# A gated cross-attention and FFN layer on one core: x kept in one ring, four PSUM banks in strict turn, normalised rows made later, and the last output projection ahead of the last FFN product

## What is computed

```python
x = x + tanh(g_xattn) * attention(layernorm(x), ctx, ctx)   # causal; projections q, k, v, o with biases
x = x + tanh(g_ffn) * (mx(layernorm(x)) @ mx(weight).T + bias)
```

## Time and profile before

| what | value |
|---|---|
| three runs: median (lowest to highest) | 1426.57 us (1426.28 to 1427.3) |
| the profiled execution | 1426.4 us |
| its span, first to last instruction | 1424.4 us |
| mean granted TensorE clock | 0.989 |
| busy: PE (matmuls), PEld (weight loads) | 1381.7 us (97%), 1220.1 us (86%) |
| busy: DVE (VectorE), ACT (ScalarE), POOL (GpSimd) | 1102.1, 894.7, 854.3 us |

### The profile page before, as it was taken

The page is one execution under the profiler, slowest core; times in us unless marked ns, Lnnn a source line. Parts: engine busy times, 40 slices in busy tenths (PEclk is TensorE's granted clock), DMA queues, the critical chain, the costliest instruction groups (busy, mean ns, idle before and its releaser), DMA issues.

```text
span 1424.4 us, 35124 instructions
## 1 busy us (share of the span) xinstructions
PE 1381.7 (97%) x10844; PEld 1220.1 (86%) x10844; DVE 1102.1 (77%) x4219; ACT 894.7 (63%) x2969; POOL 854.3 (60%) x1387
## 2 busy tenths in 40 slices
PE   6899999999999999999999999999999999999976
PEld 6788888888888888888888888888888888888865
DVE  5778787887788878778788778788778887877763
ACT  4566666666666666666666666666666666666651
POOL 2455665566665666666656566556666566666662
PEclk9999999999999999999999999999999999999988
DMA  8444434444434444434444443444443444443310
GB/s 255 107 112 106 117 93 120 115 128 107 119 90 118 118 125 118 108 94 116 118 119 124 108 114 97 116 117 128 107 119 93 115 117 125 118 111 90 86 51 29
DMA packets 156103, 159.10 MB, mean 112 GB/s; under 512 B 28176, under 2 KB 130576, under 8 KB 155920
## 3 DMA queue, kind: packets, MB, share of 16 engines
q1 hardware_dynamic: 155920, 156.87, 41.6%
HBM read 39.33 MB, written 16.78 MB: 39 GB/s over the span
## 4 chain that ended last, share of the span: by engine, by line
PE 91%; DVE 3%; SPq 2%; issue 1%; ACT 1%; POOL 1%; DMA 1%; DVEq 0%; ACTq 0%; POOLq 0%
PE proj L483 20%; PE proj L484 20%; PE proj L485 20%; PE pT_ps L533 12%; PE oT_ps L550 6%; PE proj L577 6%; PE s_ps L522 4%; PE s_ps L523 2%; SPq L342 1%; DMA all_probs<-in_L_xattn_w_v 1%; ACT all_probs L660 1%; DVE all_probs L807 0%; DMA q_stack<-q_hi 0%; POOL x L448 0%; POOL x L444 0%
## 5 line engine op out<-in xcount | busy, mean ns | idle before, releaser
L410 POOL TENSOR_TENSOR all_probs<-all_probs,rden 128x128 f32<-128x128 f32 (+1 forms) x1024 | 505.0, 514 | 473.3 <-DVE rden L867 472.1
L660 ACT ACTIVATE all_probs<-all_probs,neg_max 128x128 f32<-128x128 f32 (+1 forms) x1024 | 458.7, 451 | 396.7 <-DVE neg_max L807 396.5
L807 DVE CUSTOM_DVE_ANT_0 all_probs<-s_ps,causal 128x128 f32<-128x128 f32 (+1 forms) x1024 | 321.7, 351 | 164.4 <-PE s_ps L523 160.8
L533 PE MATMUL pT_ps<-ident,all_probs 128*128 128x128 f32 x1536 | 264.5, 282 | 6.6 <-POOL all_probs L410 4.3
L660 ACT ACTIVATION_READ_ACCUMULATOR all_probs<-all_probs,neg_max 128x1 f32 x1024 | 195.5, 191 | 0.0
L919 DVE COPY all_probs<-pT_ps 128x384 f32<-128x384 f32 x256 | 139.0, 543 | 66.5 <-PE pT_ps L533 66.5
L533 PEld LDWEIGHTS pT_ps<-ident,all_probs 128*128 128x128 f32 x1536 | 160.4, 142 | 21.7 <-issue 12.7
L522 PE MATMUL s_ps<-k_stack,q_stack 96*128 96x256 f32 x512 | 154.8, 302 | 2.8 <-DVE neg_max L807 2.2
L483 PE MATMUL proj<-cT_hi,wk_hi 128*128 128x256 f32 x512 | 153.2, 299 | 1.9 <-DVE cT_lo L861 1.1
L483 PE MATMUL proj<-aT_hi,wq_hi 128*128 128x256 f32 x512 | 148.0, 289 | 0.4 <-ACT vs L675 0.4
L484 PE MATMUL proj<-cT_lo,wk_hi 128*128 128x256 f32 x512 | 142.4, 278 | 0.0
(11 more groups left out here) (125 smaller groups left out, 3487.3 us busy)
## 6 DMA issues: line engine op xcount, KB each, us to landing
k_stack<-k_hi SPq DMA_DIRECT2D x512, 64.0 KB, 2.0
q_stack<-q_hi SPq DMA_DIRECT2D x512, 64.0 KB, 2.1
xs<-in_x SPq DMA_DIRECT2D x32, 512.0 KB, 4.2
cs<-in_ctx SPq DMA_DIRECT2D x32, 512.0 KB, 6.1
k_stack<-k_lo SPq DMA_DIRECT2D x256, 64.0 KB, 2.0
q_stack<-q_lo SPq DMA_DIRECT2D x256, 64.0 KB, 2.1
out<-x SPq DMA_DIRECT2D x32, 512.0 KB, 3.0
vs<-in_L_xattn_w_k SPq DMA_DIRECT2D x2, 512.0 KB, 7.0
```

The costliest lines, as they stand in the source:

```text
L410: last = nc.gpsimd.tensor_tensor(p, p, rden[:, sd, t, h:h + 1].to_broadcast([P, (1 + t) * P]), ALU.mult)
L533: last = nc.tensor.transpose(pT_ps[h % 2][:, m * P:(m + 1) * P], probs[:, h % P_RING, m * P:(m + 1) * P], ident[:, :])
L660: last = nc.scalar.activation(probs[:, h % P_RING, cols], probs[:, h % P_RING, cols], ACT.Exp, scale=-1.0, bias=neg_max[:, sd, t, h:h + 1] ...
L807: last = nc.vector.tensor_tensor_reduce(probs[:, h % P_RING, cols], s_ps[h % 2][:, cols], causal[:, (1 - t) * P:], 1.0, MASKED, ALU.add, A ...
```

## The change

It does four things. Lines of the changed kernel differ from those of the profile, so both are given by what they do.

1. **x in one ring.** `xs` has five places, x1 is gone, and the o unit, the FFN bias and the f product all work in the place into which x was loaded. A load of x from batch 5 on waits for the result of the batch five earlier to be written out; loads 2 to 4 wait for the last transposes of weights. The result goes out in two transfers of 256 KB, each when its half of f is added. SyncE's copies of k1 also wait for the maxima of the batch before.
2. **Four banks in strict turn.** All units, and both `weigh_values` of a batch ("av"), take the next of four banks in the order in which TensorE comes to them; each waits for the unit four turns back.
3. **xn later.** The normalised rows of batch i-1 are made in slots 2 and 3 of step i, one half in each, in place of slot 15 of step i-1. Batch 0 keeps its place.
4. **The step of the last o.** In step 34 the order is dT0 (30) in slot 1, the `weigh_values` in slot 3, dT1 (30) and o0 (31) in slot 4, o1 (31) in slot 5, f0 (30) in slot 9 and f1 (30) in slot 10.

```diff
-AV_LAG = 11
-OUT_SLOTS = ((AV_LAG + 1) % SLOTS, (AV_LAG + AV_HEADS + 1) % SLOTS)
+AV_SLOTS = (11, 3)
+AV_STEPS = (2, 3)
-BANKS = (0, 1, 2, 0, 1, 2, 0, 1, 2, 0, 1, 2, 0, 1, 0, 2)
+LAST_O = ((1, ("dT", 0)), (4, ("dT", 1)), (4, ("o", 0)), (5, ("o", 1)), (9, ("f", 0)), (10, ("f", 1)))
+BANKS = 4
-XN_SLOT = SLOTS - 1
-X_RING = 4
+XN_SLOTS = (2, 3)
+X_RING = 5
...
+    for i in range(STEPS):
+        if i == B + 2:
+            for s, (kind, half) in LAST_O:
+                work.setdefault((i, s), []).extend((kind, half, i - lag_of[kind, half], p) for p in range(PARTS[kind]))
...
+        def bank_of(kind, half, b):
+            return proj[place_of[kind, half, b] % BANKS]
+        def bank_before(kind, half, b):
+            n = place_of[kind, half, b] - BANKS
+            return taken[n] if n >= 0 else None
...
@@ SyncE, step
+                    if some(n := HEADS * (i - 2)):
+                        sp.wait_ge(max_ok, n)
                     sp.wait_ge(left["k"], 2 * (i - 2) + 2)
...
-                    if some(n := 2 * i):
-                        sp.wait_ge(xn_ok, n)
+                    if i == 1:
+                        sp.wait_ge(xn_ok, 2)
+                    elif 1 < i < X_RING:
+                        sp.wait_ge(wT_done, KC * len(WEIGHTS))
+                    elif i >= X_RING:
+                        sp.wait_ge(out_moved, 16 * T * (i - X_RING + 1))
...
-                    sp.wait_ge(left["f"], 2 * (i - 4) + 2)
-                    sp.dma_start(batch_of(out, i - 4), x1[:, side(ph, 4), :, :]).then_inc(
-                        x1_moved[side(ph, 4)], 16)
+                    for half in range(T):
+                        sp.wait_ge(left["f"], 2 * (i - 4) + half + 1)
+                        sp.dma_start(out[i - 4, half * P:(half + 1) * P, :], xs[:, place(ph, 4), half, :]).then_inc(
+                            out_moved, 16)
@@ TensorE
+            def free_bank(kind, half, b):
+                before = bank_before(kind, half, b)
+                if before and before[0] == "av":
+                    pe.wait_ge(olo_ok, 2 * before[2] + before[1] + 1)
+                elif before and before[0] == "bias":
+                    pe.wait_ge(add_ok, 1)
+                elif before:
+                    pe.wait_ge(left[before[0]], 2 * before[2] + before[1] + 1)
@@ VectorE
-                    dve.wait_ge(x1_moved[sd], 16 + 8 * b - 8 * sd)
-                    nc.vector.tensor_tensor(x1[:, sd, half, :], bank[:, :], xs[:, pl, half, :],
-                                            ALU.add).then_inc(left["o"], 1)
+                    nc.vector.tensor_tensor(x1[:, half, :], bank[:, :], x1[:, half, :], ALU.add).then_inc(left["o"], 1)
...
+                    if s in XN_SLOTS and i > 1 and live(i - 1):
+                        normal_rows(i - 1, XN_SLOTS.index(s))
```

More of the change, by code:

```diff
@@ L285, in transposed_head, with finished @@
             return lag, i - lag, (s - PT_LAG) % SLOTS
[L287 to L303, removed]
+        def finished(i, s, ago=1):
+            n = SLOTS * i + s - ago
+            for kind, half, b, part in work.get((n // SLOTS, n % SLOTS), ()):
+                if part == PARTS[kind] - 1:
+                    yield kind, half, b
+        def bank_of(kind, half, b):
[3 more added lines that the diff above has]
+            return taken[n] if n >= 0 else None
         block = es.enter_context(nc.Block())
@@ L388, in _ @@
             for_steps(step)
-            for n in range(2):
-                sp.wait_ge(x1_moved[n], 16 + 16 * (B // 2))
+            sp.wait_ge(out_moved, 16 * T * B)
         @block.gpsimd
@@ L554, in weigh_values, with unit @@
                 last.then_inc(av_done, 1)
-            def unit(u, part, kind, half, b, i):
-                bank = proj[BANKS[u]]
-                if part == 0 and (before := bank_before(u, i)):
-                    pe.wait_ge(left[before[0]], before[1])
+            def unit(kind, half, b, part):
+                bank = bank_of(kind, half, b)
+                if part == 0:
+                    free_bank(kind, half, b)
                 if part == 0 and at(b, 0) and kind in WEIGHTS:
@@ L604, in unit @@
                     last.then_inc(done[kind], 1)
-            def units(i, s):
-                for (u, part), its_slot in zip(parts, slot_of):
-                    kind, half, lag = UNITS[u]
-                    if its_slot == s and live(i - lag):
-                        unit(u, part, kind, half, i - lag, i)
             def step(i, ph):
@@ L627, in step @@
                         transpose_probs(b, h)
-                    units(i, s)
+                    for kind, half, of, part in work.get((i, s), ()):
+                        unit(kind, half, of, part)
                     for chunk in weight_chunks(i, s):
@@ L663, in exponentials, with unit @@
                 last.then_inc(p_ok, 1)
-            def unit(u, kind, half, b, sd):
-                bank = proj[BANKS[u]]
+            def unit(kind, half, b):
+                bank = bank_of(kind, half, b)
                 if kind in ("o", "f"):
@@ L674, in unit @@
                         act.wait_ge(av_done, n)
-                    nc.scalar.activation(vs[:, sd, half, :], bank[:, :], ACT.Copy).then_inc(left["v"], 1)
+                    nc.scalar.activation(vs[:, side(b, 0), half, :], bank[:, :], ACT.Copy).then_inc(left["v"], 1)
                 elif kind in ("q", "k"):
@@ L748, in step @@
                                              saturate=False).then_inc(w8_ok, 1)
[L749 to L751 removed]
+                    for kind, half, of in finished(i, s, 6):
+                        if kind == "o":
+                            to_grid(of, half)
             for_steps(step)
@@ L826, in moments, with unit @@
                                         ALU.add).then_inc(va, 1)
-            def unit(u, kind, half, b, pl, sd):
-                bank = proj[BANKS[u]]
+            def unit(kind, half, b):
+                bank = bank_of(kind, half, b)
+                x1 = xs[:, b % X_RING]
                 if kind in ("q", "k"):
```

149 lines of the change are left out of this document (80 added, 69 removed).

## The result

The changed kernel takes 1406.1 us (median of 4 runs, 1405.28 to 1409.21), the kernel before, run beside it, 1426.93 (4 runs). The ratio is 0.9858, 95% interval 0.9841 to 0.9875, so 17.8 to 22.7 us less; the forecast was 20.7 us less, 1405.7 us. The profiled execution took 1405.65 us at a span of 1403.9.

The account below looks back on a forecast made before the run. TensorE was taken as the bound, losing time to VectorE in steady steps and idling at the end. 12.5 + 1.1 + 0.4 + 4.9 + 1.2 + 0.6 = 20.7 off 1426.4 gives 1405.7 us, range 1401 to 1414.

Parts of the forecast that it names:

- Banks and xn, 0.43 a step, 12.5: Steady steps: 0.15 us from cT0's bank wait and 0.28 from k0 behind cT_lo go, 29 times; bounds 4.4 and 19.7.
- cT_lo 0.8 us early: Steady step: with xn moved, cT_lo ends near 676.1, k0 is due at 676.96, so 0.8 us to spare.
- xn hidden in slots 2 and 3: VectorE: xn's halves, the first about 0.8 us, fit its idle times of 1.19 and 1.05 us there.
- Rival D: Slots 2 and 3: xn is in the way, TensorE loses up to 1.59 us a step; 1436.8 us, chance 0.04.
- x in one ring, 0: Summing x in one ring costs nothing while its load is half a step ahead; 0, bounds -1 to 1 us.
- Start, 1.1: Step 2: k0's 1.06 us wait for cT_lo goes, step 3 gains nothing; 1.1 us, bounds 0 and 3.
- Step 32's 0.43, step 33's 0.4 and the order of step 34, 4.9: Steady gain in step 32, q1's wait for v1's bank gone in 33, reordered 34 starting dT0 (31) 4.9 us earlier.
- Tail 1.2 and last transfer 0.6: After last dT0: fewer slow matmuls if the clock stays up, 1.2 us (0 to 2.5); halved last transfer, 0.6 us.
- B: Steady steps: cT_lo stays late through ScalarE's other work, k0 keeps its 0.28 us; 1413.8 us, chance 0.10.
- C: Steady steps keep their length, only start and end gain; 1418.2 us, chance 0.07.
- E: End: the hole before o0 keeps the lower clock through both o halves, 4.8 us more; 1411.7 us, chance 0.07.
- F: Every step: units cycling through banks make the clock swing, 70 us; 1475 us, chance 0.01.

Follow-up runs that it names:

- the xn experiment: Changed kernel with both halves of xn back in slot 15, the four banks in turn kept: 1419.08 us, ratio 0.9945.
- the half xn: Changed kernel with the first half of xn back in slot 15, the second left in slot 3: 1406.03 us, ratio 0.9846.
- its run: Kernel before with only x summed in place in one ring of five, all else taken back: 1427.2 us, ratio 1.0002 (0.9993 to 1.001).
- its repetition: The changed kernel itself, unaltered, run and profiled once more: 1407.06 us, ratio 0.9853.
- the usual order: Changed kernel with the last batch's o behind f of the batch before in step 34: 1412.31 us, ratio 0.9896.
- one transfer: Changed kernel with each batch's result in one transfer of 512 KB instead of two of 256 KB: 1407.38 us, ratio 0.9856.
- the two with another end: Changed kernel with half 1's o and f (30) later in step 34: 1407.64 us; the same with nine f0 products ahead of dT1: 1407.76 us.
- the one with xn four times: Changed kernel with every half of xn computed four times in slots 2 and 3, thrice into a spare tensor: 1484.5 us, ratio 1.0393.
- the double xn: Changed kernel with every half of xn computed twice in slots 2 and 3, once into a spare tensor: 1405.83 us, ratio 0.985.

## Why the prediction was right

The time was 0.4 us from the forecast, on the forecast's own mechanisms, though two of its terms were right only as a sum. That it was as near as 0.4 us is luck: four runs of the same kernel lay 3.9 us apart.

*Banks and xn, 0.43 a step, 12.5.* Measured 0.43 to 0.46 a step and 11.8 us over 28 intervals, the first profile's 1.1 us longer one included. The sum is right, since with both stops gone both holes close. The attribution failed. The step that reads "TensorE loses 0.15 us there", as a price of its own beside xn's 0.28, took two stops on one engine for independent. With xn in slot 15 VectorE goes without a break from k_lo over xn to the maxima, ScalarE's exponentials and cT_hi wait for these, and cT_lo for cT_hi; that chain fixes when k0 can start, wherever cT0 stands. A cT0 set free 0.15 us sooner leaves its gain at k0: its change is worth 0, as the longer wait of the xn experiment shows. Behind a moved xn it is worth 0.21. The lower bound "4.4 if only the bank's wait goes" was wrong by the same reasoning; it should have been 0.

*cT_lo 0.8 us early.* It ends 0.91 us before k0. Where k0 waits for it, it ends 0.14 before (677.25 and 677.39), so 0.77 are spare, and the half xn that moved it by 0.79 used them up.

*xn hidden in slots 2 and 3.* Right, with more room than argued. The prediction carried slot 15's 0.8 us a half along; in the new place a half costs 0.44 to 0.53 us, because it no longer begins while GpSimd is at work on yz. Rival D begins somewhere between one and three further xn.

*x in one ring, 0.* Right, within the interval of its run.

*Start, 1.1.* 1.0 up to cT0 of step 4, but that place is no test: in the six profiles whose instructions are the same up to it (the change, its repetition, the usual order, one transfer, and the two with another end) it lies between 119.92 and 121.80 us. Step 2 itself shows the gain. From its cT0 to that of step 3 it is 35.6 to 36.6 us in the nine profiles with a half of xn or both later than slot 15 (without the one with xn four times), and 37.0 to 37.5 in the four with both in slot 15; the wait of 1.06 us before k0 is there in those four only. What the q copies do in step 3 differs: their wait was 0.52 before and 1.11 in the change,

```profile
99.03 0.39 PE L561 MATMUL s_ps<-k_stack,q_stack 96*128 96x256 f32 x1 [1.11 <-DMA q_stack<-q_hi]
```

but under 0.3 us in the repetition. So "nothing" for step 3 is neither borne out nor refuted.

*Step 32's 0.43, step 33's 0.4 and the order of step 34, 4.9.* Together they should put the last dT0 5.7 us closer to cT0 of step 32; it is 103.64 - 98.17 = 5.5, and 103.64 - 98.78 = 4.9 in the second profile of the same kernel. The wait of 0.43 us for v1's bank in step 33 is gone. The idle time left was 2.06 for a predicted 2.0.

*Tail 1.2 and last transfer 0.6.* 14.59 - 12.35 = 2.2 us less, of which 0.8 is the transfer and 1.4 the clock. Both sizes are 0.2 low. In the second profile of the same kernel the clock's part is 2.7, over the upper end of 2.5: by the Trainium skill, page "TensorE: Matmul & The Clock Gate", Part 1, the number of slow matmuls differs from run to run, and the two profiles agree. That the shorter idle time brings any of this gain, as the prediction had it, is not shown: with 2.06 us of it the nine profiles took 11.1 to 13.5 us from dT0 to the end, and with 7.5 to 7.7 us the three others took 12.8, and 14.4 and 14.6 with one transfer, which is 0.8 longer. So 1.4 us in one execution, beside 2.7 in the next, says little for the 1.2.

*Rivals.* B and C are out by the step of 41.82 us, D by its absence and the double xn. E did not occur in the profiled run; in the two profiles where o began at the lower clock it cost 1.7 us, about a third of E's 4.8. F is out by the clock of 1.00.

## What to carry to other kernels

Stops that one engine makes for another can hang on one chain of work, and then they don't add: before pricing each, follow the engine that is waited for from one stop to the next, and where each link between them starts as soon as the one before it is done, price only the last. Test an attribution with the edits undone singly and together; a right sum says nothing on its parts. Read the gain of a busy engine from the distance between equal starts in two steps, not from its busy time, and a helper's cost from starts of neighbours, not from recorded lengths, and in the place where it will stand: here the same work cost 1.51 us in one place and 0.97 in the other.

## What the runs showed of the hardware

VectorE's xn instruction (TENSOR_SCALAR, 128x512, fp32) takes 0.52 to 0.55 us when no GpSimd TENSOR_TENSOR is running at its start. When one is running and has over 0.3 us to go, it ends 0.28 us after that one does: so in all 302 cases in the fourteen profiles, for recorded lengths of 0.6 to 1.5 us (0.278 to 0.287 us after). The 773 with none running took 0.517 to 0.551.

Once to five times in a run a step is 0.2 to 1.1 us longer. In the three cases looked at, in two profiles of the changed kernel, it is a transfer that stacks k; here the chain of waits of the first, whose step 10 took 42.91 us:

```profile
380.41 3.80 DMA k_stack<-k_lo
```

ScalarE then waited for it 2.7 us to overwrite k_hi. What delays the transfer stays open, but the place is not random: step 10 is longer in three profiles (42.91, 42.59 and, with one transfer, 42.54 us), and step 5 in five of those with a usual step of 41.82 (42.1 to 42.9). The four or five runs of one kernel lie 1.6 to 5.8 us apart; these longer steps, the clock at the end and the start's 1.9 us are of that size, and so are the smaller edits here, so these are told only by their own places in the profile.

How fast the clock comes back at the end differs between executions of the same instructions (11.05 and 12.35 us for the same tail), and in two profiles it came back only during the last o. Nothing in the edits says which execution it will be. Whether a shorter idle time alone raises it is not settled: with 7.7 us of it, the kernel with the usual order in step 34 took 12.8 us from there to the end, inside the 11.1 to 13.5 us of those with 2.06.
